# A planned graph-network kernel: the weights and first loads enter the plan, six units instead of seven, six staging places instead of three

## The reference

```python
x = _layernorm(x + L0(x, adj))   # 12 heads of 32: softmax(q k^T / sqrt(32) + beta*adj, masked where adj == 0) v
x = _layernorm(x + L1(x, adj))   # twice: delta = exp(u_left/u_right by triangle) * adj; h = relu(norm(delta/sum @ (h W_lin)))
x = _layernorm(x + L2(x, adj))   # twice: delta = softmax(h h^T / sqrt(384)) * adj, upper, diagonal and lower part
                                 #        each times its own projection (hl, hs, hr); relu(norm(...))
x = _layernorm(x + L3(x, adj))   # 12 heads: softmax(q k^T * scale + adj) v, then @ Wo.T + bo
```

## Time and profile before

| what | value |
|---|---|
| median of 3 runs | 2942.34 us (2942.23 to 2944.7) |
| the profiled execution | 2937.27 us, its span 2935.5 us |
| mean granted clock of PE | 0.985 of full |
| PE, DVE, ACT, POOL busy | 2824.7, 2286.8, 1858.1, 1336.6 us |
| DMA | 237.41 MB, mean 81 GB/s |

### The profile page before, as it was taken

The page is one execution under the profiler, slowest core; times in us unless marked ns, Lnnn a source line. Parts: engine busy times, 40 slices in busy tenths (PEclk is TensorE's granted clock), DMA queues, the critical chain, the costliest instruction groups (busy, mean ns, idle before and its releaser), DMA issues.

```text
span 2935.5 us, 93395 instructions
## 1 busy us (share of the span) xinstructions
PE 2824.7 (96%) x35008; PEld 2091.3 (71%) x35008; DVE 2286.8 (78%) x8566; ACT 1858.1 (63%) x4885; POOL 1336.6 (46%) x2571
## 2 busy tenths in 40 slices
PE   4899999999999999999999999999999999999994
PEld 3666777777777777777777777777777777777762
DVE  5867787787787787787787787887787787887874
ACT  4655666666666666666666666666666666666653
POOL 1334454444444454454444454454454454444442
PEclk8899999999999999999999999999999999999997
DMA  6524444444454454444444454444444454454432
GB/s 172 122 47 70 79 86 74 78 86 76 77 87 76 76 87 73 78 87 76 77 88 74 79 87 75 80 83 75 82 83 77 79 85 75 78 87 78 73 61 52
DMA packets 803991, 237.41 MB, mean 81 GB/s; under 512 B 771544, under 2 KB 803416, under 8 KB 803424
## 3 DMA queue, kind: packets, MB, share of 16 engines
q1 hardware_dynamic: 796208, 218.87, 42.7%
q10 hardware_dynamic: 7344, 12.58, 1.4%
HBM read 29.99 MB, written 12.58 MB: 15 GB/s over the span
## 4 chain that ended last, share of the span: by engine, by line
PE 84%; DMA 7%; DVE 6%; ACT 1%; issue 1%; POOL 1%; SPq 1%; DVEq 0%; POOLq 0%; ACTq 0%
PE bank L776 11%; PE bank L777 10%; PE bank L778 10%; PE bank L764 9%; PE bank L765 8%; PE bank L766 8%; PE bank L868 7%; DMA turned<-flat 6%; PE bank L813 4%; PE bank L782 3%; PE bank L861 3%; PE bank L798 2%; PE bank L799 2%; PE bank L800 2%; PE bank L824 1%
## 5 line engine op out<-in xcount | busy, mean ns | idle before, releaser
L764 PE MATMUL bank<-turned,w_hi 128*128 128x128 f16 x4608 | 818.7, 221 | 10.9 <-DMA turned<-flat 7.6
L765 PE MATMUL bank<-turned,w_hi 128*128 128x128 f16 x4608 | 816.3, 220 | 0.0
L766 PE MATMUL bank<-turned,w_lo 128*128 128x128 f16 x4608 | 816.1, 220 | 0.0
L776 PE MATMUL bank<-w_hi,turned 128*128 128x384 f16 x2112 | 696.1, 330 | 34.8 <-DMA turned<-flat 33.8
L777 PE MATMUL bank<-w_lo,turned 128*128 128x384 f16 x2112 | 695.9, 330 | 0.0
L778 PE MATMUL bank<-w_hi,turned 128*128 128x384 f16 x2112 | 695.9, 329 | 0.0
L682 ACT ACTIVATE ab<-bank 128x384 f16<-128x384 f32 (+1 forms) x768 | 373.8, 487 | 304.3 <-PE bank L766 190.2
L691 ACT ACTIVATE score<-score,small 128x128 f32<-128x128 f32 x1536 | 500.9, 391 | 94.4 <-DVE small L951 91.7
L586 POOL TENSOR_TENSOR flat<-score,flat 128x384 f16<-128x384 f32 x256 | 234.5, 916 | 575.9 <-ACT flat L697 575.7
L764 PEld LDWEIGHTS bank<-turned,w_hi 128*128 128x128 f16 x4608 | 455.4, 99 | 47.6 <-DMA turned<-flat 15.9
L765 PEld LDWEIGHTS bank<-turned,w_hi 128*128 128x128 f16 x4608 | 452.8, 98 | 9.4 <-issue 1.6
(11 more groups left out here) (116 smaller groups left out, 6428.4 us busy)
## 6 DMA issues: line engine op xcount, KB each, us to landing
turned<-flat SPq DMA_TRANSPOSE x960, 2.8
x<-x_dram SPq DMA_DIRECT2D x64, 192.0 KB, 2.3
out_dram<-score SPq DMA_DIRECT2D x64, 192.0 KB, 2.3
w_stage<-w_dram ACTq DMA_DIRECT2D x18, 576.0 KB, 4.4
adj<-adj_dram SPq DMA_DIRECT2D x64, 64.0 KB, 2.2
rows<-rows_dram ACTq DMA_DIRECT2D x1, 1920.0 KB, 7.1
w_stage<-w_dram SPq DMA_DIRECT2D x1, 576.0 KB, 6.7
turned<-bias_dram SPq DMA_DIRECT2D x4, 9.0 KB
```

The costliest lines, as they stand in the source:

```text
L764: pe.matmul(dst, lhsT=w_hi[:, w, k, cols], rhs=t_hi[u][:, k, :], start=(k == 0), stop=False)
L765: pe.matmul(dst, lhsT=w_hi[:, w, k, cols], rhs=t_lo[u][:, k, :], start=False, stop=False)
L766: last = pe.matmul(dst, lhsT=w_lo[:, w, k, cols], rhs=t_hi[u][:, k, :], start=False, stop=(k == DT - 1 and w not in BIAS_OF))
L776: pe.matmul(dst, lhsT=t_hi[u][:, k, :], rhs=w_hi[:, w, k, :], start=(k == 0), stop=False)
```

## The change

`UNITS` becomes 6 and `STAGES` 6. The weights' steps, the loads into places that have to come free, the constant rows and the biases become steps of the plan with their own costs (`ONCE`), and a weight's load waits for the split of the weight that had its place. The first six loads are all issued by ACT at the start. The first units' loads and masks get times in the plan, SP's `load_weight` is gone, DVE and POOL no longer wait for beta at their start (the first mask does). In the first 60 us of the plan a transpose is taken to be 1 us later. Each of the first ten and last twelve units gets a shift of its wanted times (`SHIFTED`). All of `PARTS`' wanted times are new, and a few costs: a score group on PE 0.36 for 0.28, a transpose on SP 1.24 for 1.35.

```diff
-UNITS = 7
+UNITS = 6
...
-PERIOD = 43.143
+PERIOD = 43.413
+
+SHIFTED = {0: -157.05, 1: -10.17, 2: 0.92, 3: 0.34, 4: 11.49, 5: 5.57, 6: -2.21, 7: -9.92, 8: -5.83, 9: -0.10, 52: -0.18, 53: -0.39, 54: 2.32, 55: -16.90, 56: -10.74, 57: -16.00, 58: -14.66, 59: 13.38, 60: -11.18, 61: 5.30, 62: -30.74, 63: -106.08}
...
-    (PE, "scores", 0): (56.14, 0.280, 0.460, ((VECTOR, "project", 0), (VECTOR, "project", 1), (VECTOR, "project", 2)), ()),
...
+    (PE, "scores", 0): (204.78, 0.360, 0.540, ((VECTOR, "project", 0), (VECTOR, "project", 1), (VECTOR, "project", 2)), ()),
...
-STAGES = 3
+STAGES = 6
...
-WEIGHTS_FROM, WEIGHT_EVERY, LOAD_EVERY = 5.5, 4.4, 10.0
+ROWS_AFTER = 6
+LOAD_FROM, LOAD_EVERY, BETA_AT = 2.2, 1.6, 9.0
+
+CROWDED = 60.0
+FIRST = -1e6
+
+
+ONCE = {(SCALAR, "biases", 0): (FIRST + 0.5, 8.0, 1.1, 1.2, ()),
+        (VECTOR, "biases", 0): (FIRST + 0.5, 0.0, 1.95, 2.1, ((SCALAR, "biases", 0),)),
+        (SCALAR, "load_rows", 0): (FIRST + ROWS_AFTER + 0.3, 0.0, 0.5, 10.0, ((SCALAR, "weight", WEIGHT_ORDER[ROWS_AFTER]),))}
+for n, w in enumerate(WEIGHT_ORDER):
+    if n >= STAGES:
+        ONCE[SCALAR, "load_weight", n] = (FIRST + n - STAGES + 0.4, 0.0, 0.5, 5.2, ((VECTOR, "weight", WEIGHT_ORDER[n - STAGES]),))
+    ONCE[SCALAR, "weight", w] = (FIRST + n, 0.0 if n >= STAGES else 6.6 + 2.5 * n, 1.1, 1.25,
+                                 ((SCALAR, "load_weight", n),) if n >= STAGES else ())
+    ONCE[VECTOR, "weight", w] = (FIRST + n, 0.0, 1.3, 1.45, ((SCALAR, "weight", w),))
+TRANSPOSES = [part for part in PARTS if part[0] == SYNC and part[1] in ("turn", "scores")]
...
+    for i in range(B):
+        for part, (at, _, _, after, after_last) in PARTS.items():
+            wanted[part, i] = i * PERIOD + SHIFTED.get(i, 0.0) + at
+            comes_after((part, i), *((p, i) for p in after))
+            if i >= UNITS:
+                comes_after((part, i), *((p, i - UNITS) for p in after_last))
+        for w in WEIGHT_ORDER:
+            comes_after(((PE, "project", w), i), ((VECTOR, "weight", w), 0))
...
+        comes_after(((POOL, "bias_x", 0), i), ((SCALAR, "load_rows", 0), 0))
+        comes_after(((VECTOR, "inner", 0), i), ((SCALAR, "load_rows", 0), 0))
+    for i in range(UNITS):
+        soonest[(SYNC, "load", 0), i] = LOAD_FROM + LOAD_EVERY * i - (0.9 if i else 0.0)
+        soonest[(VECTOR, "masks", 0), i] = BETA_AT
...
+        if part in TRANSPOSES and now < CROWDED:
+            until += 1.0
...
             load(0, 0)
-            load_weight(sp, 0)
...
-            for n in (1, 2):
+            for n in range(STAGES):
                 load_weight(act, n)
...
-                if n == 3:
-                    act.dma_start(rows[:, :, :], rows_d.rearrange("r d -> (r d)").partition_broadcast(128)
-                                  .rearrange("p (r d) -> p r d", d=D)).then_inc(rows_loaded, 16)
-                if 0 < n <= NW - STAGES:
-
-                    act.wait_ge(w_lo_made, n)
-                    load_weight(act, n + STAGES - 1)
+
+            def next_weight(i, n):
+
+                act.wait_ge(w_lo_made, n - STAGES + 1)
+                load_weight(act, n)
+
+            def load_rows(i, k):
+                act.dma_start(rows[:, :, :], rows_d.rearrange("r d -> (r d)").partition_broadcast(128)
+                              .rearrange("p (r d) -> p r d", d=D)).then_inc(rows_loaded, 16)
...
+                if (k, i) == first(VECTOR, "masks"):
+                    dve.wait_ge(beta_loaded, 16)
+                    dve.tensor_scalar(minus_beta[:, :], beta[:, :], -1.0, None, ALU.mult).then_inc(minus_beta_made, 1)
+                    dve.wait_ge(minus_beta_made, 1)
...
-            dve.wait_ge(beta_loaded, 16)
-            dve.tensor_scalar(minus_beta[:, :], beta[:, :], -1.0, None, ALU.mult).then_inc(dve_consts, 1)
             dve.wait_ge(dve_consts, DVE_CONSTS)
```

More of the change, by code:

```diff
@@ new lines @@
+    (SYNC, "turn", 3): (385.56, 1.240, 3.150, ((POOL, "turn", 3),), ()),
+    (SYNC, "turn", 4): (392.41, 1.240, 3.150, ((VECTOR, "turn", 4),), ()),
+    (PE, "attend", 5): (392.81, 0.234, 0.454, ((SYNC, "scores", 5),), ()),
+    (POOL, "bias_x", 0): (395.44, 0.920, 1.050, ((POOL, "turn", 0),), ()),
+    (SCALAR, "project", 15): (401.05, 0.400, 0.567, ((PE, "project", 15),), ()),
+    (PE, "project", 16): (401.18, 1.517, 1.697, ((SYNC, "turn", 5),), ()),
+    (VECTOR, "inner", 0): (402.20, 1.370, 1.565, ((PE, "mix", 0),), ()),
@@ L266, in plan, with comes_after @@
[L266 to L270 removed]
+    followers, missing, soonest, wanted = defaultdict(list), Counter(), defaultdict(float), {}
+    def comes_after(node, *others):
+        for other in others:
+            followers[other].append(node)
+            missing[node] += 1
@@ L271, in plan @@
+    for part, i in wanted:
+        if not missing[part, i]:
+            ready[part[0]].append((wanted[part, i], part, i, soonest[part, i]))
     order, free = {engine: [] for engine in ready}, {engine: 0.0 for engine in ready}
     done, holder, banks = {}, [None] * BANKS, {}
-    left = sum(map(len, ready.values())) + sum(n > 0 for n in missing.values())
-    while left:
+    for _ in wanted:
         freed = sorted((done.get(h, 1e9) if h else -1.0, b) for b, h in enumerate(holder))
@@ L287, in plan @@
         ready[engine].remove(chosen)
-        left -= 1
         order[engine].append((part[1], part[2], i))
-        if part not in PARTS:
-            free[engine] = now + WEIGHT_COST[part[1], engine]
-            continue
-        _, busy, until, _, _ = PARTS[part]
+        busy, until = ONCE[part][2:4] if part in ONCE else PARTS[part][1:3]
+        if part in TRANSPOSES and now < CROWDED:
+            until += 1.0
         free[engine] = now + busy
```

407 lines of the change are left out of this document (193 added, 214 removed).

## The result

The changed kernel is slower: 2952.1 us median (2950.6 to 2958.0, 7 runs) beside 2939.2 for the kernel before on the same chip (2937.9 to 2944.7, 7 runs). The ratio is 1.0044, 95% interval 1.0033 to 1.0055. I had forecast 2925 and a range that ended at 2948.

A forecast was written before the change was run, and what follows sets the result against it. TensorE was taken as the bound, with almost nothing to win in the middle and the losses at both ends. Head -13, six units +5 and tail -9 gave -17 on the profiled 2937.3; median forecast 2925, range 2902 to 2948.

The forecast's parts named there:

- Head, first part (0): Up to unit 0's project 3, at 98 us: 59.9 us lost against 60.0, so no change (-7 to +9).
- I take 44, nearer the row's flat rate: Head, weights' block: ACT's second eviction at 44 us, between ends of 38 and 53, with loads at 390 GB/s.
- the wall's 54: Rival, head: weight transfers and waits for free places bring the second eviction to 54; +10 or more, 2935 to 2940; chance 0.15.
- I keep 48: Head: from unit 0's first exp to its project 3 stays 48 us (47.9 before), with four units' rounds as the chain.
- Head, second part (-13): From project 3 to 240 us: 6 us lost to idle time and low clock instead of 19 (-17 to -4).
- Six units (+5): Middle: six units for seven leave less slack; late transposes cost 0.09 us more per unit over 57 units (0 to +23).
- All still fit, by 0.4 to 4 us: Middle, six units: chains such as scores to attend and last projection to scores 4 still fit the work between them.
- six units stall the middle: Rival, middle: short chains make it slower, deciding from 0.39 us per unit; 2954 at 0.6; chance 0.15.
- From 2800 to that mix: From 2800 us to unit 63's last mix: PE idle 4.8 now, only one short pair of 0.9 in the new order; -2.
- Tail (-7): After unit 63's last mix: units 61, 63 and 62 march together; 69.3 us with 30.7 of work, 38.6 lost for 45.8.
- plus 6: Tail: 6 us added to unit 62's chain of 58.6 because three units share the same engines.
- PE's own time per unit changes with the order: Whole kernel: named as one way the forecast would be wrong, priced by no row of the earlier profile.

The follow-up runs named there:

- experiment 6: Changed kernel, three weight loads first, three behind the first weight, itself ahead of unit 1's turn: 2953.6 us; that swap in the old kernel with new head: 2935.7.
- Experiments 4 and 5: Changed kernel: 4, POOL's bias_x left out 2939.6 us, one step later 2950.2; 5, score group 3 earlier, with later bias 2945, also ACT's project 10 eviction earlier.

## Why the prediction was wrong

The measured time is 27 us over the forecast. In profiled spans the sum was -17 and came out at +14.9, 32 us apart, and by columns these are: 19 ahead of the tail, where the prediction had no term; 11 in the middle; 9 in the head; and 6 the other way in the tail.

- **Head, first part (0): right by luck, two wrong terms cancelled.** Project 3 of unit 0 came at 98.95 for 98, with 60.8 lost for 59.9. But the step "I take 44, nearer the row's flat rate" failed: the second eviction came at 51.5, near the other end of 53 and the wall's 54. The flat 390 GB/s of the earlier trace rows belongs to a few us; over the block, with units' loads and transposes between them, the engines were full at 313. ("ACT starts on weights at about 8.4" was wrong too, 13.20, but experiment 6 shows that this did not count.) Against it "I keep 48" from the first exp to project 3 was too long by 8: 39.6 from 59.37. The prediction had named the likely reason, nine us of ACT's time on weights that the new rounds do not have, and priced it at nothing; no run tests it alone. It had also concluded from the page's rule on turns by the packet (the Trainium skill, DMA: Bandwidth & Descriptors, Queues, rings and completion order) that the first transposes would be protected from queued weights. The row has the changed kernel's transposes in its first 30 us; the one of the kernel before in that time took 2.9. The longest, 10.6, also stood behind three units' loads on SP's own queue, the last of which landed at 16.5 us, 1.8 ahead of it; but the last one, issued at 23.75 when SP's own loads had landed and with one transpose ahead of it, still took 5.4. So no full protection is seen, and the rule itself is neither shown nor refuted.

```profile
DMA to landing us min/median/max: 4.6/5.0/10.6
```

- **Head, second part (-13): nearly right where it ended, and given back later, 9 us short.** At 200 us of work the changed kernel had lost 69.9 and the kernel before 81.0, a gain of 11. At 395 it was 80.7 and 84.9, a gain of 4. From 240 to 300 us PE idles 2.6 of 60 and the clock is at 0.97, with 1.2 us at one turn_adj. My sum stopped at 240 us, and nothing in it asked whether the units that started together had reached the middle's spacing by then. "Rows and beta 0" was not tested apart.
- **Six units (+5): the wrong mechanism, and 16 instead of 5.** "All still fit, by 0.4 to 4 us" failed. I had compared distance and chain for scores to attend and for the last projections to scores 4, and these do fit: late landings cost little. I had not done it for scores 3 to turn_adj, whose distance went from 2.98 us to 0.65 with 1.0 needed, and project 10 to mix 2, 8.1 to 2.1. Both numbers stand in the two orders and could be read before any run. The rival "six units stall the middle" had the sign and named the wrong places; its point of decision, 0.39 us per unit, is about what came (16.0 over 44 units is 0.36). (The "286.1 us of other work" of that paragraph and the 242.0 hold the unit's own 43 us as well; their difference, which is all that was used, is right.) Experiments 4 and 5 show the first of the two waits by length; for the second, the edit that removed it cost more than it gave. What the step from seven units to six costs by itself stays open, since the table changed with it.
- **Ahead of the tail (no term): the step that failed most, 18.6 us.** The sum goes from the middle's +5 to "From 2800 to that mix", and nothing was counted between. Its -2 was about right in its own place: from 2800 to unit 63's last mix PE idles about 1 us for 4.8. But the shifts start at unit 52, from 2224 us of work on PE's order is another one than without them, and from 2300 it has no period. The two runs on the shifts show that the loss is theirs, and that the ten small ones carry 12 of 17; through which single steps, I did not settle. PE's waits from 2400 to 2800 in the changed kernel are many small ones at different lines:

```profile
PE bank L789 <- DMA turned<-flat: 2.5, 3, 1.3
PE bank L849 <- DMA turned<-flat: 2.2, 3, 1.3
PE bank L893 <- DVE score L1033: 2.0, 4, 1.1
PE bank L801 <- DVE ab L958: 1.8, 1, 1.8
```

- **Tail (-7): right in kind, 3 us too small.** From the end of unit 63's last mix (2883.9) to the end of the span are 66.5 us, for the 69.3 forecast; with its 30.7 of work that is 35.8 lost, 10 less than before (the other 5 of the column's 15.5 lie ahead of that mix). Two steps were off, one each way. Unit 62's mix ended 7.8 us behind unit 63's, not 4.7: it waited 1.8 for VectorE and took 3.8 for 2.0 at a clock of 0.78. And behind it came 58.6 us, as long as unit 63's chain alone before, so of the "plus 6" for three units on the same engines nothing is seen:

```profile
2884.00:2891.80 7.80, 5.98 (x32) 2.77 (x33) 4.98 (x17) 3.50 (x8) 4.83 (x10) 0.78 0.22 42
2891.80:2950.40 58.60, 33.50 (x471) 23.33 (x471) 34.11 (x145) 31.07 (x87) 25.31 (x38) 0.76 0.43 80
```
- **My own test in the text, "PE's own time per unit changes with the order", is not what happened:** the excess is waits of 0.1 to 0.4 us, so short that more than half of it lies within matmuls' recorded durations (turn_adj 328 ns for 273 before). From 500 to 2300 us PE is idle 15.0 us for 8.6 before, and of the three places the list of waits shows only these:

```profile
PE bank L893 <- ACT ab L707: 5.6, 31, 0.3
PE bank L858 <- DVE small L974: 0.6, 2, 0.4
```

## What to carry to other kernels

When a table or planner writes a new order, compare for **every** dependent pair of steps the work written between them with the length of its chain (here 1.28 us from a score group to the step behind VectorE, read in one timeline), not only for the pairs that were slow before, and for every stretch of the order, also where it leaves its period; one pair that is 0.36 us short costs 15 us in 41 units. A gain at the start has to be followed until the steady order is reached. A short distance is not repaired by moving one step later: what was behind it or covered by it moves too, so of seven local edits here two helped, and only together.

## What the hardware showed that I had not expected

VectorE's gain, whose two large inputs lie in SBUF, does not run beside a POOL step on SBUF of the same size, it queues behind it. Alone the gain takes 0.61 us. It took 0.99 when it started 0.42 us into a POOL step of 1.00, and 1.28 in the rows below, where the POOL step behind took 1.32 for its usual 1.00. VectorE's row, then POOL's:

```profile
1079.72 1.28 DVE L1064 SCALAR_TENSOR_TENSOR z<-score,small,rows 128x384 f32<-128x384 f32 x1
```

```profile
1079.67 0.91 POOL L598 TENSOR_TENSOR flat<-x,flat 128x384 f16<-128x384 f32 x1
1080.54 1.32 POOL L604 TENSOR_TENSOR x<-x,rows 128x384 f32<-128x384 f32 x1
```

The Trainium skill (SBUF — State Buffer, Who interferes with whom) says that a VectorE instruction with two inputs in SBUF contends with a GpSimd instruction that reads SBUF, over a pair of ports that only one of the two can hold. The rows agree within 0.2 us: 0.58 left of the POOL step and 0.61 of its own would be 1.19 for the 0.99 measured. So it is throughout: of the 256 gains of the changed kernel 123 began within a POOL step, and in the median they took 0.20 us less than that sum. In the kernel before no gain was hit from 500 to 2300 us (641 ns at most), and few in all of it; the new order put 61 us of such queueing on the gain. It cost next to nothing in the middle (2.4 us came back there without the bias, and nothing with the bias moved), where PE's distances were the bound, and up to 9 us from 2300 us of work on, where leaving out the bias (which also takes load off POOL) returned them.
